# Selection steps one unit later in each engine's order, and the banded attention's first loads ahead of its constants

## The reference, cut to what matters

```python
# banded attention of layer 1: 8 heads per side, window of 16 keys around each position
dots = jnp.einsum('bhdt,bhdtw->bhtw', qh, k_win) * scale
attn = jax.nn.softmax(dots, axis=-1)
out = jnp.einsum('bhtw,bhdtw->bhdt', attn, v_win)
x = x + tanh(g_xattn[1]) * (Wo @ out + bo)
# selection of layer 1: which tokens and which output columns of the last layer count
dots = jax.nn.softmax(layernorm(x) @ centroids.T / 0.1, axis=-1)   # 64 clusters
hits = dots > 0.01
query_sel = jnp.any(hits, axis=1)                # per token
row_sel = jnp.any(hits, axis=0)[assignments]     # per output column
```

## Time and profile before

| what | value |
|---|---|
| median of 3 runs | 2182.61 us |
| the profiled execution, its own time | 2183.45 us |
| its span, first to last instruction | 2181.7 us |
| mean granted clock of PE | 0.954 of full speed |
| busy share of the span | PE 91%, DVE 49%, ACT 30%, POOL 17% |
| the stage, between barriers | about 1527 to 1992 us |
| waits of PE in 1600 to 1942 us, longest group | 19.0 us in 14 waits, for ACT `se_xn` |

### The profile page before, as it was taken

The page is one execution under the profiler, slowest core; times in us unless marked ns, Lnnn a source line. Parts: engine busy times, 40 slices in busy tenths (PEclk is TensorE's granted clock), DMA queues, the critical chain, the costliest instruction groups (busy, mean ns, idle before and its releaser), DMA issues. The chain is left out here.

```text
span 2181.7 us, 50890 instructions
## 1 busy us (share of the span) xinstructions
PE 1979.2 (91%) x20126; PEld 1596.3 (73%) x20126; DVE 1069.1 (49%) x1866; ACT 660.6 (30%) x1114; POOL 370.4 (17%) x341
## 2 busy tenths in 40 slices
PE   6999689999995999999996799998698989986998
PEld 6999689999994777777774477776366666664887
DVE  5444231121113555555553555553678777854443
ACT  2222131111101443444432111121366656652000
POOL 0000000000005310111110000000465555640000
PEclk9999899999996999999998899999699999996999
DMA  4332434443347454445532345544755344423442
GB/s 149 117 115 97 174 116 167 148 143 114 113 162 303 181 202 185 174 184 213 212 126 88 112 169 183 185 175 164 185 145 146 117 140 124 124 80 110 145 147 90
DMA packets 149429, 328.60 MB, mean 151 GB/s; under 512 B 56432, under 2 KB 82672, under 8 KB 141104
## 3 DMA queue, kind: packets, MB, share of 16 engines
q1 hardware_dynamic: 147344, 326.04, 42.4%
q10 hardware_dynamic: 1952, 0.60, 0.1%
HBM read 200.25 MB, written 125.83 MB: 149 GB/s over the span
## 5 line engine op out<-in xcount | busy, mean ns | idle before, releaser
L1499 ACT ACTIVATE a_pt<-a_st_bank 128x1024 f32<-128x1024 f32 x128 | 131.1, 1024 | 267.9 <-PE a_st_bank L1545 267.9
L1051 POOL TENSOR_TENSOR a_sm<-a_sm,a_nmax 113x1024 f32<-113x1024 f32 x84 | 159.1, 1901 | 113.8 <-DVE a_nmax L1101 113.8
L1451 DVE TENSOR_REDUCE a_nmax<-a_s_bank 128x8 f32<-128x1024 f32 x128 | 156.5, 1223 | 27.6 <-PE a_s_bank L1533 21.2
L268 PE MATMUL q_qb<-q_xt_hi,wq_hi 128*128 128x256 f32 x512 | 146.2, 286 | 3.0 <-DVE wq_lo L179 3.0
L268 PE MATMUL kv_kb<-kv_ct_hi,wk_hi 128*128 128x256 f32 x512 | 144.9, 283 | 3.0 <-DVE wv_lo L179 3.0
L268 PE MATMUL q_qb<-q_xt_lo,wq_hi 128*128 128x256 f32 x512 | 145.6, 284 | 0.0
L268 PE MATMUL q_qb<-q_xt_hi,wq_lo 128*128 128x256 f32 x512 | 145.6, 284 | 0.0
L268 PE MATMUL kv_kb<-kv_ct_hi,wk_lo 128*128 128x256 f32 x512 | 144.9, 283 | 0.0
L268 PE MATMUL kv_kb<-kv_ct_lo,wk_hi 128*128 128x256 f32 x512 | 144.9, 283 | 0.0
L1228 PE MATMUL a_s_bank<-a_ks,a_qs 64*49 64x256 f32 x1344 | 98.2, 408 | 32.3 <-DMA a_ks<-k 20.2
L1095 DVE TENSOR_TENSOR a_sm<-a_s_bank,a_band 113x1024 f32<-113x1024 f32 x84 | 102.8, 1224 | 42.8 <-PE a_s_bank L1228 41.8
(11 more groups left out here) (203 smaller groups left out, 4517.1 us busy)
## 6 DMA issues: line engine op xcount, KB each, us to landing
a_qs<-q SPq DMA_DIRECT2D x32, 1024.0 KB, 5.4
a_ks<-k SPq DMA_DIRECT2D x32, 1024.0 KB, 7.2
k<-kv_raw SPq DMA_DIRECT2D x32, 512.0 KB, 4.5
f_xin<-x SPq DMA_DIRECT2D x32, 512.0 KB, 4.7
a_vraw<-v SPq DMA_DIRECT2D x32, 304.0 KB
q_xin<-in_x SPq DMA_DIRECT2D x16, 512.0 KB, 5.8
q<-q_out_lo SPq DMA_DIRECT2D x16, 512.0 KB, 3.6
q<-q_out_hi SPq DMA_DIRECT2D x16, 512.0 KB, 4.3
```

The costliest lines, as they stand in the source:

```text
L268: m = pe.matmul(out, a(x, c), b(y, c), start=(i + j == 0), stop=(len(terms) * j + i == n - 1))
L1051: pool.tensor_tensor(sm[live, k], sm[live, k], nmax[live, k, :].unsqueeze(2).to_broadcast([LIVE, 16, KEYS]), ALU.add).then_inc(shifted, 1)
L1451: dve.tensor_reduce(to, s_bank[:].rearrange("p b (h x) -> p b h x", h=4), X, ALU.max, negate=True).then_inc(maxed, 1)
L1499: act.activation(pt[:, s % 2], st_bank[:].rearrange("p b (h x) -> p (b h) x", h=4), ACT.Exp).then_inc(expd, 1)
```

## The change

The lists of the engines get a new order. `turn_rows` goes from lead 2, last in its step, to lead 1, behind `score` and `project` of the next step; `logits` from the middle of a step to the head of the next; `rows_out` from ahead of `exponential` to behind it; `lowest` from behind `divide` to the head of the next step; SP's `store_xt` from lead 1 to lead 0, behind the q and k load. At the start, SP issues the first q and k before the band and the constants, and waits only for slot 0 of `a_ks`, which DVE and POOL now zero by halves; slot 1, `a_vraw` and the constants each have their own wait where they are used. The one-hot matrix is made in DVE's step -8 and not ahead of step -12.

```diff
         @block.sync
-            sp.dma_start(band[:], e.i["band"]).then_inc(const, 16)
-            for dst, src in (... five constants ...):
-                sp.dma_start(dst, src).then_inc(w_in, 16)
             sp.wait_ge(pads[0], 2)
-            sp.wait_ge(pads[1], 1)
             def load(u, s, i):
                     sp.wait_ge(scored, done(u - s + last(g - 2)))
+                    if slot:
+                        sp.wait_ge(pads[1], 1)
             def load_values(u, s, i):
                     sp.wait_ge(v_ready, 2 * (t - 1) + START)
+                    sp.wait_ge(pads[2], 1)
-            def load_weights(s):
+            def others(s):
+                if s == -16:
+                    sp.dma_start(band[:], e.i["band"]).then_inc(const, 16)
+                if s == -14:
+                    for dst, src in (... five constants ...):
+                        sp.dma_start(dst, src).then_inc(w_in, 16)
                 r = s + NC
                 if r >= 0:
                     sp.dma_start(raw[:, r, :], e.i["WfT1"][r * P:(r + 1) * P, :]).then_inc(raw_in[r], 16)
-            staggered(sp, N, PER, [(3, each(store_x3)), (1, each(store_xt)), (17, load), (15, load_values),
-                                   (9, each(load_x2))], opening=load_weights)
+            staggered(sp, N, PER, [(3, each(store_x3)), (0, each(store_xt)), (17, load), (15, load_values),
+                                   (9, each(load_x2))], opening=others)
         @block.gpsimd
+            pool.memset(ks[:, 0, 2:4], 0.0).then_inc(pads[0], 1)
+            pool.memset(qs[:, :, D:DPAD], 0.0).then_inc(pads[3], 1)
+            pool.memset(vraw[:], 0.0).then_inc(pads[2], 1)
             pool.memset(mark[:], 0.0)
-            pool.memset(vraw[:], 0.0).then_inc(pads[1], 1)
-            pool.memset(qs[:, :, D:DPAD], 0.0).then_inc(pads[1], 1)
         @block.vector
-            for k in range(2):
-                dve.memset(ks[:, k], 0.0).then_inc(pads[0], 1)
+            dve.memset(ks[:, 0, 0:2], 0.0).then_inc(pads[0], 1)
+            dve.memset(s_bank[:], 0.0)
+            dve.memset(o_bank[:], 0.0).then_inc(ps_zeroed, 1)
             (three small copies into order)
-            dve.memset(s_bank[:], 0.0)
-            dve.memset(o_bank[:], 0.0).then_inc(ps_zeroed, 1)
+            dve.memset(ks[:, 1], 0.0).then_inc(pads[1], 1)
-            dve.wait_ge(w_in, 80)
-            (onehot copy, compare, gbo)
+            def clusters(s):
+                if s != -8:
+                    return
+                dve.wait_ge(w_in, 80)
+                (onehot copy, compare, gbo)
-            staggered(dve, N, PER, [(12, mask), (12, maximum), (7, divide), (3, each(moments)), (1, each(lowest)),
-                                    (0, each(choose))])
+            staggered(dve, N, PER, [(0, each(lowest)), (12, mask), (12, maximum), (7, divide), (3, each(moments)),
+                                    (0, each(choose))], opening=clusters)
         @block.scalar
-            act.wait_ge(prep, 2)          (now inside projected)
-            staggered(act, N, PER, [(1, each(rows_out)), (10, exponential), (0, each(chances)), (2, each(normalise)),
+            staggered(act, N, PER, [(10, exponential), (2, each(normalise)), (1, each(rows_out)), (0, each(chances)),
                                     (9, turn_out), (5, attention_out), (4, each(projected)), (8, value_out)])
         @block.tensor
-            pe.wait_ge(pads[1], 2)
-            pe.wait_ge(zeroed, 1)
-            pe.wait_ge(w_in, 80)          (now inside project)
+            pe.wait_ge(pads[3], 1)
-            staggered(pe, N, PER, [(12, score), (4, project), (5, turn_attention), (9, turn), (1, each(logits)),
-                                   (8, value), (7, turn_back), (2, each(turn_rows))])
+            staggered(pe, N, PER, [(0, each(logits)), (12, score), (4, project), (1, each(turn_rows)), (5, turn_attention),
+                                   (9, turn), (8, value), (7, turn_back)])
```

More of the change, by code:

```diff
@@ L927, in attend1_select @@
         x_bank = ps("se_x_bank", [P, 2, 512])
-        const = sem("a_const"); zeroed = sem("a_zeroed"); pads = [sem(f"a_pads{k}") for k in range(2)]; ps_zeroed = sem("a_ps_zeroed"); go = sem("a_go")
+        const = sem("a_const"); zeroed = sem("a_zeroed"); pads = [sem(f"a_pads{k}") for k in range(4)]; ps_zeroed = sem("a_ps_zeroed"); go = sem("a_go")
         qk_in = [sem(f"a_qk_in{k}") for k in range(2)]
@@ L961, in _ @@
             begin(sp, *x3_out, *xt_out)
-            sp.dma_start(band[:], e.i["band"]).then_inc(const, 16)
-            for dst, src in ((wt[:], e.i["WT1"][:, 3, :]), (b[:], e.i["b1"]), (iota[:], e.i["iota"]),
-                             (assign, e.i["assign"].partition_broadcast(NCL)),
-                             (cent[:], e.i["centT"].rearrange("(c p) n -> p c n", p=P))):
-                sp.dma_start(dst, src).then_inc(w_in, 16)
             sp.wait_ge(pads[0], 2)
-            sp.wait_ge(pads[1], 1)
             def load(u, s, i):
@@ L1009, in store_xt @@
                 sp.dma_start(e.xT[t], xt[:, k]).then_inc(xt_out[k], 16)
-            def load_weights(s):
+            def others(s):
+                if s == -16:
+                    sp.dma_start(band[:], e.i["band"]).then_inc(const, 16)
+                if s == -14:
+                    for dst, src in ((wt[:], e.i["WT1"][:, 3, :]), (b[:], e.i["b1"]), (iota[:], e.i["iota"]),
+                                     (assign, e.i["assign"].partition_broadcast(NCL)),
+                                     (cent[:], e.i["centT"].rearrange("(c p) n -> p c n", p=P))):
+                        sp.dma_start(dst, src).then_inc(w_in, 16)
                 r = s + NC
@@ L1081, in _ @@
             dve.memset(ones[:], 1.0)
-            dve.wait_ge(w_in, 80)
[L1083 to L1087, removed]
             dve.wait_ge(const, 16)
             scores = s_bank[live].rearrange("p b (h x) -> p (b h) x", h=8)
+            def clusters(s):
+                if s != -8:
+                    return
+                dve.wait_ge(w_in, 80)
+                dve.tensor_copy(onehot[:], assign).then_inc(prep, 1)
+                dve.wait_ge(prep, 1)
+                dve.tensor_scalar(onehot[:], onehot[:], iota[:, 0:1], None, ALU.is_equal)
+                dve.tensor_tensor(gbo[:], b[:, 3:4], e.gate[:, 1:2], ALU.mult).then_inc(prep, 1)
             def mask(u, s, i):
@@ L1155, in _ @@
             begin(act, expd, ev_t, ev_o, a_out, o_out, normed, x_out, chance)
-            act.wait_ge(prep, 2)
             def exponential(u, s, i):
@@ L1182, in projected @@
             def projected(t, g, k, nth):
+                act.wait_ge(prep, 2)
                 act.wait_ge(o_mm, done(t))
@@ L1211, in _ @@
             pe.wait_ge(ps_zeroed, 1)
-            pe.wait_ge(pads[1], 2)
-            pe.wait_ge(zeroed, 1)
-            pe.wait_ge(w_in, 80)
+            pe.wait_ge(pads[3], 1)
             def score(u, s, i):
@@ L1277, in project @@
                     if last(g) == s:
+                        pe.wait_ge(w_in, 80)
                         pe.wait_ge(a_out, done(u))
```

## The result

After the change the median is 2165.9 us (4 runs, 2161.94 to 2168.02), beside 2181.86 for the kernel before. The ratio is 0.9924, with a 95% interval of 0.9910 to 0.9938; 2166 was forecast. The span went from 2181.7 to 2166.2 us; the mean granted clock stayed at 0.954.

What follows compares the result with a forecast made beforehand. PE was taken to set the pace, busy for 90.18 of 100 us in a steady stretch. Terms: 13.3 + 6.1 - 2.5 = 16.9 us off the profiled 2183.45, so a median of 2166 us, range 2158 to 2174.

Steps and rivals of the forecast that it cites:

- Part 1: Steady batches on PE: `score` ahead of `turn_rows` fills the wait for `se_xn`; 1.02 us in 13 batches, 13.3 us gained.
- The loop's return: PE's two gaps where its loop branches back, 6.9 us: effect of the new order unknown, 3 us either way.
- The drain: Last two batches: they keep their chain, the fourteenth wait for `se_xn` stays, nothing gained.
- Part 2: Stage start: halved memsets on DVE and POOL let q load and first score come sooner; 6.1 us gained (5.3 to 6.1).
- the gap of 0.82 us: Stage start, behind DVE's first memset: may belong to that memset, which would leave a gain of 5.3 us.
- Part 3: Fill: the one-hot matrix now stands ahead of the fifth unit's mask on DVE; 2.5 us lost (0.65 to 4.5).
- the reading of the earlier trace: Fill: a DVE operation beside POOL's shift stands still until the shift is over; next `score` 2.5 us late.
- at face: Fill: one-hot operations on DVE take only the times they took alone; `score` 0.65 us late.
- C: Steady batches: the wait for `se_xn` returns as one for mask or `rows_out`, only the start gains; 2179 us, chance 0.08.
- D: Steady batches: `rows_out` behind `exponential` comes late and delays `logits`; 6 us slower, 2189 us, chance 0.05.
- A: Fill: order gains as forecast, start gives nothing, one-hot matrix costs 4.5 us with the clock; 2169 to 2174, chance 0.15.
- B: PE's gap in the fill goes or the loop-return gaps shrink; 2158 to 2161 us, chance 0.14.

Runs made afterwards that it cites:

- e2: The kernel before with the five new engine lists and its old start: 2167.35 us, ratio 0.9942.
- e0: The changed kernel run again with no edit: 2166.25 us, ratio 0.9934 to the kernel before.
- e1: The changed kernel with the five old engine lists, so only the new start: 2176.49 us, ratio 0.9985 to the kernel before.
- e5: The changed kernel with the one-hot matrix made in `lowest` of the last batch, not in the fill: 2161.59 us, ratio 0.9915 to the kernel before.
- e7: The changed kernel with the one-hot matrix in the drain and PE's loop written out: 2152.76 us, ratio 0.9874 to the kernel before.
- e8: The kernel before with the new lists of PE and DVE, but the old ones of SP and ACT: 2172.07 us, ratio 0.9959.

## Why the prediction was right

*Part 1* held in mechanism and size: 1.01 to 1.07 us per batch, as forecast, 13.3 us for 13 batches, and 12.6 in the times of e2. `se_xn` and `turn_rows` kept their distance, and the score went into the gap. What the prediction did not see is that the other moves are part of that price. It said that `logits` have 0.1 to 0.2 us to spare at their new place and never asked what they would have at the old one: 0.33 us too little. Whoever takes `turn_rows` alone gets 0.53.

*The loop's return* was put at 0, with 3 us either way. The gaps themselves grew by 0.9 to 1.5 us with the new order, and with the slow clock behind them the two spacings move by 3.7 us between two executions of the same kernel. So the distance from the first to the fourteenth `turn_rows` is no sharp test of the 13.3: it fell by 10.4 to 14.9 us, depending on which traces of before and after are taken. The clean spacings and the time of e2 carry that term. *The drain*, put at nothing, became 0.8 us shorter.

*Part 2*: 6.1 to 6.8 us between the two traces of before and the three of a new start (after, e0, e1), against 6.1 (5.3 to 6.1). SP issues q 0.03 us behind the memset's end, as it did before, so the gap of 0.82 us took nothing off. That it is not less than forecast has a reason that the prediction did not have: DVE's first memset now begins 0.51 us behind POOL's and not 0.95. And the transfers are not quite the same: from q's issue to the first score it is 5.26 to 5.89 us, and 5.50 and 5.42 before.

*Part 3*: right at its place, by the reading of the earlier trace rows and not at face: the compare, started at 1556.33, ended at 1558.60, 0.54 us behind POOL's shift, and the next score came 1.9 to 2.1 us late. The Trainium skill has in "SBUF — State Buffer", section "Who interferes with whom", that a VectorE instruction in a two-port mode, which a cast or a tensor_scalar can enter, shares a port pair with GpSimd: the first to issue holds it for its whole instruction, and the other is blocked. The trace agrees with it in both directions: the compare, behind POOL's shift, took 2.27 us against 0.74, and the shift, behind the cast, 2.27 against 1.90. But the term is not simply a loss. With the one-hot matrix gone (e5, e7) the fill kept its length within what its gaps and clock move. The start alone brought 3.4 us, with 6.1 - 2.5 = 3.6 forecast; with an interval of 1.1 to 5.2 us, and a fill that moves by more than the term, that close a match is in part luck.

*The rivals.* C (the wait comes back) fell: `score` waits 0.3 us. D (`rows_out` late behind `exponential`) fell: `logits` wait for nothing, and e8, with the old ACT list, is no faster. A and B named the gaps without a releaser and the clock behind them, and these do move, by 3 to 4 us between executions, but to neither side in the median.

## What to carry to other kernels

Where an engine waits for a result with the next unit's work queued behind it, put that work ahead of the wait; the gain is the work's own length, as long as the wait covers it, and the consumer of the late result has to be moved as well, or it takes part of the gain. A gap that names no releaser is still a gap with a cause: it was tried here by two edits, and with the one-hot matrix moved they were worth about as much again as the change. And compare stages by their own first and last instruction, since one span holds some 7 us that come from elsewhere.

## What the runs showed of the hardware

- At the return of PE's hardware loop, with a body of 21 units, PE stood for 3.3 to 5.0 us (22 returns), and the mean granted clock of the 9 us after it was 0.62 to 0.83. Written out, both were gone: 10.2 us for two returns. In each such gap a 16 KB transfer of the `instruction` queue began, and PE went on 1.6 to 1.9 us after its end.
- In the fill, code that runs once, four steps of PE took 16.3 to 20.4 us while the eight weight loads ran, and 14.2 without them.
- A tensor_scalar of DVE beside POOL's tensor_tensor: 2.27 us and not 0.74, and POOL's own 2.27 and not 1.90. Small operations of POOL beside a cast and a tensor_scalar of DVE (e5): 0.56 and 0.81 us and not 0.19 and 0.55. The time stands in the instruction's duration, not as a wait.
- With unchanged code ahead of it, the stage started anywhere within 7 us; two executions of the same kernel were 3.6 us apart (after and e0). The latest two had a granted clock of 0.96 ahead of it, the others 0.97.
